# An attention and channel-mix block: denominators moved next to the values, x loaded in eight parts, and another opening

## What is computed

```python
h = _layernorm(x)                                  # (64, 256, 512)
qs, ks, vs = relu(h), relu(ctx), relu(ctx)         # as (b, t, 16 heads, 32)
att = softmax(einsum('bthf,byhf->bhty', qs, ks) / sqrt(32))
out = einsum('bhty,byhf->bhtf', att, vs)           # (b, 16, 256, 32)
out = out.reshape(bs, ts, -1)                      # reshaped as it lies, heads outermost
x = x + tanh(g_xattn) * relu(out @ ffn_w.T + ffn_b)
h = _layernorm(x); h_prev = h shifted by one token
xr = mu_r * h + (1 - mu_r) * h_prev;  xk = mu_k * h + (1 - mu_k) * h_prev
x = x + tanh(g_ffn) * sigmoid(xr @ W_r) * (square(relu(xk @ W_k)) @ W_v)
```

## Time and profile before

| | |
|---|---|
| median of 3 runs | 2743.56 us (2736.8 to 2748.57) |
| profiled execution | 2753.73 us, of which the span of instructions is 2751.9 |
| granted TensorE clock, mean | 0.99 of full speed |
| busy: TensorE matmul | 2651.8 us (96%) |
| busy: VectorE | 2299.0 us (84%) |
| busy: ScalarE | 1757.6 us (64%) |
| busy: GpSimd | 1140.8 us (41%) |
| DMA | 576.72 MB, mean 210 GB/s |

### The profile page before, as it was taken

One profiled execution on the slowest core, in us unless ns is written; L12 is line 12 of the kernel. 1 busy time (PEld: TensorE's weight loads), 2 busy tenths in 40 slices (PEclk: granted clock), 3 DMA queues, 4 the chain that ended last, 5 costly groups with the idle time before them and its releaser, 6 DMA issues. The chain is left out here.

```text
span 2751.9 us, 65467 instructions
## 1 busy us (share of the span) xinstructions
PE 2651.8 (96%) x20354; PEld 2058.2 (75%) x20354; DVE 2299.0 (84%) x4109; ACT 1757.6 (64%) x3531; POOL 1140.8 (41%) x902
## 2 busy tenths in 40 slices
PE   3799999999999999999999999999999999999998
PEld 2477777777777777777777777777777777777776
DVE  5678888888888888888888888888888888888774
ACT  4466566666666666666666666666666666666553
POOL 0144444434544434444444444444444444443434
PEclk9799999999999999999999999999999999999999
DMA  8667677777777777777777778778777777777641
GB/s 255 195 185 220 184 229 221 204 231 219 210 228 217 208 227 219 209 221 226 204 219 227 211 212 236 210 207 235 214 205 230 219 204 231 222 204 224 177 139 45
DMA packets 510927, 576.72 MB, mean 210 GB/s; under 512 B 178976, under 2 KB 410400, under 8 KB 510880
## 3 DMA queue, kind: packets, MB, share of 16 engines
q1 hardware_dynamic: 357552, 340.92, 43.5%
q10 hardware_dynamic: 153328, 235.20, 29.0%
HBM read 373.56 MB, written 201.33 MB: 209 GB/s over the span
## 5 line engine op out<-in xcount | busy, mean ns | idle before, releaser
L574 ACT ACTIVATE probs<-bank 128x512 f32<-128x512 f32 x1024 | 604.7, 596 | 480.3 <-PE bank L1045 456.5
L808 DVE TENSOR_REDUCE m_nat<-bank 128x2 fp32r<-128x512 f32 x1024 | 686.8, 681 | 103.0 <-PE bank L1033 102.8
L1033 PE MATMUL bank<-k_st,q_st 96*128 96x256 f32 x2048 | 438.0, 296 | 14.0 <-DVE m_nat L808 5.3
L1045 PE MATMUL bank<-q_st,k_st 97*128 97x256 f32 x2048 | 426.1, 290 | 12.5 <-DMA q_st<-m_t 11.9
L1045 PEld LDWEIGHTS bank<-q_st,k_st 97*128 97x128 f32 x2048 | 357.8, 191 | 90.9 <-issue 28.2
L1033 PEld LDWEIGHTS bank<-k_st,q_st 96*128 96x128 f32 x2048 | 359.7, 193 | 76.3 <-ACT bank L586 15.8
L399 POOL TENSOR_TENSOR o_lo<-o_mv,o_hi 128x512 fp32r<-128x512 f32 x128 | 201.7, 1576 | 512.1 <-ACT o_hi L595 512.1
L830 DVE RECIPROCAL o_val<-bank 128x256 f32<-128x256 f32 x192 | 336.2, 1751 | 60.7 <-PE bank L1071 56.4
L586 ACT ACTIVATE bank<-bank,m_nat 128x256 f32<-128x256 f32 x512 | 227.5, 444 | 180.3 <-DVE m_nat L808 180.3
L1088 PE MATMUL bank<-xk_hi,w_hi 128*128 128x256 f32 x1024 | 296.0, 289 | 1.0 <-DVE th L893 1.0
L1088 PE MATMUL bank<-xk_hi,w_lo 128*128 128x256 f32 x1024 | 287.9, 281 | 0.0
(11 more groups left out here) (94 smaller groups left out, 6151.8 us busy)
## 6 DMA issues: line engine op xcount, KB each, us to landing
q_st<-q_dram ACTq DMA_DIRECT2D x256, 256.0 KB, 4.7
k_st<-k_dram SPq DMA_DIRECT2D x256, 256.0 KB, 4.3
x_ln<-x_dram SPq DMA_DIRECT2D x256, 128.0 KB, 4.1
k_raw<-ctx_t_dram SPq DMA_DIRECT2D x256, 128.0 KB, 4.9
q_st<-q_dram ACTq DMA_DIRECT2D x256, 128.0 KB, 2.5
k_st<-k_dram SPq DMA_DIRECT2D x256, 128.0 KB, 4.8
o_dram<-o_val SPq DMA_DIRECT2D x256, 128.0 KB, 2.2
o_mv<-o_dram SPq DMA_DIRECT2D x512, 64.0 KB, 2.1
```

The costliest lines, as they stand in the source:

```text
L574: nc.scalar.activation(probs[:, n // GR % 2, n % GR, :, :].rearrange("p v t -> p (v t)"), st_bank[n % 2][:, :], ACT.Exp).then_inc(exp_read ...
L808: nc.vector.tensor_reduce(m_nat[:, c % 2, n % GR, :], s_bank[n % 2][:, :].rearrange("p (u y) -> p u y", u=NU), AX_X, ALU.max, negate=True) ...
L1033: mm = nc.tensor.matmul(s_bank[n % 2][:, T * u:T * u + T], q_st[0:QK, c, g, P * u:P * u + P], k_st[0:QK, c, g, :], start=True, stop=True)
L1045: mm = nc.tensor.matmul(st_bank[n % 2][:, T * v:T * v + T], k_st[0:ST, c, g, P * v:P * v + P], q_st[0:ST, c, g, :], start=True, stop=True)
```

## The change

1. `denominators` moves next to `values` in groups 0, 2 and 3. In group 3 the transpose of the maxima now follows both, in group 0 it goes ahead of both. In group 2 `scores(i + 1, 4)` goes ahead of the values, and the denominators, which stood one `shifted_scores` later, come up; the transpose follows them. VectorE's copy of that transpose goes behind `head_max(i + 1, 4)`.
2. `load_x` has eight loads of 16 partitions with two rows each in place of four of 64 partitions with one. The order of the queries within a remainder changes with it, so that `o_high` and `o_low` read runs of 16 neighbours of `o_mv` instead of every fourth element. For the first sequence half of the eight go to ScalarE's queue.
3. The opening (i from -2 to 0) of SyncE is written out. The weights' loads are spread: 0 to 3 at i = -2, 4 to 7 one by one at i = 0. The splits are spread over i from -1 to 1 (`split_high(i, n, when)` works at i = when), the loads of x1, of the bias and of the first v and a small setup step of VectorE come later, and TensorE waits for two halves at iteration 1 and for all at iteration 2.

```diff
                     after(sp, x_normed, NU * b)
-                    for m in range(GR):
-                        part = slice(P // 2 * (m % 2), P // 2 * (m % 2) + P // 2)
-                        sp.dma_start(x_ln[part, m // 2, :],
-                                     x[b].rearrange("(r m) d -> m r d", m=GR)[m]).then_inc(x_loaded, 16)
+                    for m in range(1 if first_sequence(b) else NU):
+                        for k in range(KC):
+                            row = P // 2 * m + P // 8 * k
+                            sp.dma_start(x_ln[row:row + P // 8, :, :],
+                                         x[b].rearrange("(a k u m) d -> k m a u d", k=KC, u=NU, m=NU)[k, m]
+                                         ).then_inc(x_loaded, 16)
             def load_k(b):
...
                     sp.dma_start(out[b, P * u:P * u + P, :], x1[:, par, u, :]).then_inc(stored, 16)
+            def opening(i, par):
+                if i == -2:
+                    load_k(0)
+                    load_w(range(0, 4))
+                    load_x(1)
+                    write_k(0, par)
+                elif i == -1:
+                    stack_k(0, 0, 1 - par)
+                    stack_k(0, 1, 1 - par)
+                    load_k(1)
+                    move_m(0, 0)
+                    stack_k(0, 2, 1 - par)
+                    load_x(2)
+                else:
+                    stack_k(0, 3, par)
+                    move_m(0, 1)
+                    load_w(range(4, 5))
+                    write_k(1, 1 - par)
+                    move_m(0, 2)
+                    load_w(range(5, 6))
+                    keys_written(1)
+                    stack_k(1, 0, 1 - par)
+                    load_k(2)
+                    move_m(0, 3)
+                    load_w(range(6, 7))
+                    write_o(0, 0)
+                    stack_k(1, 1, 1 - par)
+                    load_x(3)
+                    write_o(0, 1)
+                    stack_k(1, 2, 1 - par)
+                    move_m(1, 0)
+                    load_w(range(7, 8))
+                    read_o(0, 0)
+                    write_k(2, par)
+                    write_o(0, 2)
             def iteration(i, par):
+                if isinstance(i, int) and -2 <= i <= 0:
+                    opening(i, par)
+                    return
                 stack_k(i, 3, par)
...
                 load_k(i + 2)
-                load_w(i, range(0, 6), -2)
-                if not (isinstance(i, int) and i == 0):
-                    move_m(i, 2)
+                move_m(i, 2)
                 write_o(i, 0)
                 stack_k(i + 1, 1, 1 - par)
-                if not (isinstance(i, int) and i == -1):
-                    load_x(i + 3)
+                load_x(i + 3)
                 move_m(i, 3)
                 write_o(i, 1)
-                if not (isinstance(i, int) and i == -1):
-                    stack_k(i + 1, 2, 1 - par)
+                stack_k(i + 1, 2, 1 - par)
                 move_m(i + 1, 0)
-                if isinstance(i, int) and i == -1:
-                    stack_k(i + 1, 2, 1 - par)
-                    load_x(i + 3)
-                load_w(i, range(6, 8), -1)
                 read_o(i, 0)
-                if not (isinstance(i, int) and i == -1):
-                    write_k(i + 2, par)
+                write_k(i + 2, par)
                 write_o(i, 2)
...
                     after(pool, z_ready, NU * (b - 1) + u + 1)
-                    nc.gpsimd.tensor_tensor(by_tile(o_lo, u), o_mv[:, :, :].rearrange("p g (a k) -> p k g a", k=KC),
+                    nc.gpsimd.tensor_tensor(by_tile(o_lo, u), o_mv[:, :, :].rearrange("p g (k a) -> p k g a", k=KC),
                                             by_tile(o_hi, u).bitcast(F32), ALU.subtract).then_inc(o_lo_ready, 1)
...
         def _(act):
+            for k in range(KC):
+                row = P // 2 + P // 8 * k
+                act.dma_start(x_ln[row:row + P // 8, :, :],
+                              x[0].rearrange("(a k u m) d -> k m a u d", k=KC, u=NU, m=NU)[k, 1]
+                              ).then_inc(x_loaded, 16)
             act.dma_start(mu_sb[:, 0, :], mu[0]).then_inc(setup_loaded, 16)
...
                     after(act, stored, 16 * (b - 1))
+                    if first_sequence(b):
+                        act.wait_ge(w_lo_ready, 4)
                     act.dma_start(x1[:, par, :, :], x[b].rearrange("(u p) d -> p u d", p=P)).then_inc(x1_loaded, 16)
...
                     after(act, z_ready, NU * (b - 1) + u + 1)
-                    nc.scalar.activation(by_tile(o_hi, u), o_mv[:, :, :].rearrange("p g (a k) -> p k g a", k=KC),
+                    nc.scalar.activation(by_tile(o_hi, u), o_mv[:, :, :].rearrange("p g (k a) -> p k g a", k=KC),
                                          ACT.Copy).then_inc(o_hi_ready, 1)
...
                 exponent(i, 1)
+                split_high(i, 6, 1)
                 sum_exp(i, 7)
                 exponent(i, 2)
+                split_high(i, 7, 1)
                 kt_relu(i - 2, 0)
...
                 stack_q(i + 1, 0, 1 - par)
+                split_high(i, 0, -1)
+                split_high(i, 1, -1)
                 exponent(i, 4)
...
                     xr_high(i - 2)
-                split_high(i, 0, -2)
+                load_bias(i)
                 exponent(i, 6)
-                split_high(i, 1, -2)
+                weights_split(i)
                 z_relu(i - 1, 0)
...
                 stack_q(i + 1, 1, 1 - par)
-                load_first_v(i)
-                split_high(i, 5, -1)
                 exponent(i, 8)
...
                 ka_high(i - 2, 1)
-                split_high(i, 6, 0)
-                split_high(i, 7, 0)
                 exponent(i, 9)
...
                 q_halve(i + 2)
+                split_high(i, 2, -1)
+                split_high(i, 3, -1)
                 exponent(i, 10)
+                split_high(i, 4, 0)
                 r_tanh(i - 2, 0)
...
                 stack_q(i + 1, 2, 1 - par)
+                load_first_v(i)
                 exponent(i, 12)
+                split_high(i, 5, 0)
                 xk_high(i - 1, 0)
...
                 o_high(i, 0)
-                split_high(i, 2, -2)
-                split_high(i, 3, -2)
-                split_high(i, 4, -2)
             pipeline(act, iteration)
...
                 head_max(i, 10)
+                split_low(i, 6, 1)
                 invert(i)
...
                 norm_1(i + 2)
-                split_low(i, 0, -2)
-                split_low(i, 1, -2)
-                split_low(i, 4, -1)
-                split_low(i, 5, -1)
+                split_low(i, 0, -1)
+                split_low(i, 1, -1)
+                split_low(i, 7, 1)
                 head_max(i, 12)
...
                 head_max(i + 1, 1)
-                q_low(i + 2)
+                if not (isinstance(i, int) and i == -1):
+                    q_low(i + 2)
                 head_max(i + 1, 2)
...
                 head_max(i + 1, 3)
-                copy_m(i + 1, 0)
+                if isinstance(i, int) and i == -1:
+                    copy_m(i + 1, 0)
+                    q_low(i + 2)
                 k_low(i + 2)
+                split_low(i, 4, 0)
                 head_max(i + 1, 4)
+                if not (isinstance(i, int) and i == -1):
+                    copy_m(i + 1, 0)
                 finish(i - 2, 0, par)
...
                 head_max(i + 1, 6)
-                split_low(i, 2, -2)
-                split_low(i, 3, -2)
-                split_low(i, 6, 0)
-                split_low(i, 7, 0)
-            dve.wait_ge(setup_act, 2)
-            nc.vector.tensor_scalar(tgh[:, :], tg[:, 1:2], 0.5, None, ALU.mult).then_inc(setup_dve, 1)
-            dve.wait_ge(setup_dve, 1)
+                split_low(i, 2, -1)
+                split_low(i, 3, -1)
+                split_low(i, 5, 0)
             pipeline(dve, iteration)
...
             def weights_split(i):
-                if isinstance(i, int) and i == 1:
+                if isinstance(i, int) and i == 2:
                     pe.wait_ge(w_hi_ready, 8)
                     pe.wait_ge(w_lo_ready, 8)
+                if isinstance(i, int) and i == 1:
+                    pe.wait_ge(w_hi_ready, 2)
+                    pe.wait_ge(w_lo_ready, 2)
                     for u in range(NU):
...
                 values(i - 1, 3)
+                denominators(i - 1, 3)
                 turn(0)
-                denominators(i - 1, 3)
                 dense(0, 1)
...
                 dense(2, 3)
+                turn(1)
                 values(i, 0)
-                turn(1)
                 denominators(i, 0)
...
                 dense(6, 2)
+                scores(i + 1, 4)
                 values(i, 2)
+                denominators(i, 2)
                 turn(7)
-                scores(i + 1, 4)
                 dense(6, 3)
...
                 scores(i + 1, 5)
-                denominators(i, 2)
                 dense(7, 1)
```

31 lines of the change are left out of this document (17 added, 14 removed).

## The result

The changed kernel takes 2897.3 us (median of 4 runs, 2885.0 to 2902.8), the kernel before 2746.1 in the same comparison: a ratio of 1.0545, with a 95 % interval of 1.051 to 1.058. The prediction said 2670 and gave 0.04 to slower. The profiled execution of the changed kernel took 2885.0 us, its span 2883.2.

A forecast was written before the change was run, and what follows sets the result against it. TensorE's own stream was taken to bound the steady part (busy 398.16 of 400 us). 57.6 us from joined products plus 16 from the opening made 74 less: 2680 from the profiled 2753.7, median 2670, range 2640 to 2708 (0.72).

The forecast's parts named there:

- (b): SyncE's `read_o(i, 0)` and ScalarE's `o_high` come 1.8 us later, harmless since dense(2, 0) uses the product much later.
- (e): Chain from group 3's `norm_o` over `o_dram` to `o_lo`: 0.40 us slack used up, query order gives 0.5 us.
- The query order's part: `o_high` on ScalarE falls from 1.137 to 0.64 us, giving chain (e) 0.5 us; nothing counted for `o_lo`.
- The terms of the sum: TensorE's joined products 0.90 us a sequence, 57.6 us in 64, plus the opening's 16: 74 us less.
- Groups 0 and 3: Denominators joined to values on TensorE save 0.22 us in group 0 and 0.36 in group 3 per sequence.
- Group 2: Denominators that stand alone on TensorE cost 1.20 us, joined to values 0.88: 0.32 us saved per sequence.
- The opening: TensorE's first waits shrink: 5.5 us for weights, 5.7 for `m_t`, 4.8 for VectorE's splits; 16 us, bounds 5 and 25.
- (a): Move of the next sequence's group-0 maxima (`m_t`) goes out later but lands in time, 3.1 us left; the tightest step.
- (c): Group 3's transpose comes later, at 1213.5, but VectorE copies it only at 1214.29, after `finish`: no loss.
- (d): Group 0's transpose needs head 11's maximum, which VectorE takes before `norm_1` and head 12's maximum: no loss.
- Rival 3: The x loads hold up SyncE's move of group 3's maxima; slower, about 2811 us if 2.2 us late; chance 0.05.
- Rival 1: Group 0's `m_t` lands late and TensorE waits each sequence, giving the gain back: about 2728 or 2696; chance 0.10.

The follow-up runs named there:

- b4: a4 with VectorE's copy of the group-0 maxima behind `k_low` and the maximum of head 4, as in the changed kernel: 2920.0 us, 1.061.
- b3: Changed kernel with `read_o(i, 0)` in front of the move of the next group-0 maxima on SyncE, instead of behind it: 2650.2 us, 0.964.
- c1: Kernel before with `read_o(i, 0)` behind `write_k(i + 2)` on SyncE instead of in front of it: 2993.4 us, 1.086.
- d1: b3 with `write_k(i + 2)` moved behind `write_o(i, 2)` on SyncE: 2869.7 us, 1.045.
- e2: Kernel before with `write_k(i + 2)` moved behind `write_o(i, 2)` on SyncE, nothing else changed: 3014.3 us, 1.098.
- c3: Changed kernel with ScalarE's loads of `q_st` of group 0 and x1 moved behind `o_high(i - 1, 1)`: 2787.3 us, 1.014.
- d3: c3 with the store of the result also moved behind `read_o(i - 1, 1)` on SyncE: 2709.1 us, 0.987.
- e1: Changed kernel with write_k writing only group 0's quarter of the keys (256 KB for 1 MB) in the steady loop: 2864.7 us, 1.043.
- d2: Changed kernel with `write_k(i + 2)` in front of the move and `read_o(i, 0)` still behind it: 2893.2 us, 1.053.
- a2: Kernel before with the eight x loads and the natural query order alone: 2740.1 us, 0.998.
- a4: Changed kernel with group 2 alone put back, VectorE's copy included: 2697.8 us, 0.983.
- c2: Kernel before with the changed order of the three groups and `read_o(i, 0)` in front of the move: 2672.4 us, 0.973.
- d4: b3 with the four x loads and the old query order put back: 2668.7 us, 0.970.

## Why the prediction was wrong, step by step

**The step that failed is (b):** "`read_o(i, 0)` stands behind that move and comes 1.8 us later, so ScalarE's `o_high` does too; its product is used a good part of an iteration later, by dense(2, 0)." The lateness was right (1.9 us on average, against group 3's values), and so was its first user on TensorE. What I left out is everything else that hangs on the read. GpSimd's `o_low` of tile 0 is late, and VectorE's `norm_o` of group 3 waits for it before it may write `o_val` (`o_mv` is one buffer for both tiles). And write_k stands behind the read in SyncE's program, so that its 1 MB lies nearer to group 3's way over `o_dram`. In the kernel before, `o_low` of tile 0 ended at 1213.37 and `norm_o` began at 1214.59: 1.2 us of slack against a step 1.8 later, in rows that I could have read.

Shown: VectorE's late copy alone, which makes the move, the read and write_k late, brings the whole loss (b4); the exchange that brings read and write_k forward takes it away (b3). Each of the two brings a loss of that size by itself, the late read in c1 and the late write_k in d1 and e2. TensorE's wait for `o_lo`, the form that the loss has in the changed kernel, is write_k's by the table above, with ScalarE's loads and the store beside it (188 us with all three moved away: c3, d3). Taking write_k's bytes away (e1) left a loss of nearly the same size, which the rows put to VectorE beside GpSimd. So the losses replace each other, and how the 247 us divide between the late read and the late write_k in the order as changed stays open (d2, the run meant for it, brought a wait of its own).

**(e), the slack of the chain.** I took the slack of 0.40 us, had the chain's start on VectorE 0.5 us earlier and the transfers' times as fixed. The write of `o_val`, behind that start, came 0.5 us later on average, and the transfers took 3.1 us more, by the means of the table. The query order's part was right in kind: with b3's order the eight loads and the query order together are worth 18 us (2668.7 to 2650.2), while with the old TensorE order they are worth 6 (a2).

**The terms of the sum** are measured in b3, where nothing is given back. Forecast 74 us, measured 97. On average between 400 and 2400 us a sequence takes 40.96 us before, 40.44 in a4 and 39.78 in b3 (one copy of `rden` to the next). Groups 0 and 3: 0.58 us forecast, 0.52 measured. Group 2: 0.32 forecast, 0.66 measured. At its place the joined run saves 0.33, as forecast. Another 0.28 is at the border of two sequences, where two products of scores took 0.42 and 0.34 us from start to start (0.43 and 0.33 before), and in b3 0.24 each; a4 first, then b3:

```profile
1258.53 0.40 PE L1096 MATMUL bank<-q_st,k_st 97*128 97x256 f32 x2
1258.95 0.50 PE L1084 MATMUL bank<-k_st,q_st 96*128 96x256 f32 x2
```

```profile
1278.12 0.40 PE L1098 MATMUL bank<-q_st,k_st 97*128 97x256 f32 x2
1278.36 0.41 PE L1086 MATMUL bank<-k_st,q_st 96*128 96x256 f32 x2
```

No wait is named there, and the cause wasn't tried. The 1.18 us a sequence make 76 us in 64, where I had 57.6. The opening: 16 forecast. The fourth copy of `rden` comes 17.0 us sooner in b3 than before (169.73 against 186.74), 3.5 of them from three shorter sequences: 13.5. Between c2 and d4, which differ by the opening alone, it is 9.3 at that point and 3.7 in the whole time; where the rest goes wasn't followed.

**(a)** held in the changed kernel and in b3: no wait for the move of `m_t` stands in their steady part. **(c)** and **(d)** held as well: in b3 TensorE is busy for all of the 2000 us from 400 on. **Rival 3** didn't come: eight issues took about 4 us (5.0 forecast), and the next move landed in time. The rule of the Trainium skill on back-pressure that I set beside it is stated there of transfers between cores, and nothing here shows it at work. **Rival 1** came in d2 (111.9 us), and in part in c3 (34.6 us).

**The chances.** 0.92 for faster rested on a list of late steps in which one was waved through by its TensorE user. The forecast of slower had no mechanism for a step that is late on SyncE and short of its slack on VectorE and close to other transfers in the queues.
